# Router logits from column-tiled fp32 matmuls and one transposition, in a sandwich of linear attention and a gated expert layer

## The chip, the cores and the metric

The kernel runs on one core of one Trainium2 chip. The metric is the device time of one execution in microseconds (us); lower is better. Engines are named as the profile names them: PE is TensorE's matmul stream and PEld its weight loads, DVE is VectorE, ACT is ScalarE, POOL is GpSimd, SP issues the DMAs.

## The reference, cut to what matters

Input is x of 2 x 4096 tokens with 256 features. The first half adds a chunked linear attention, the second a layer of 8 experts weighted by a router. The part that the change touches is the router:

```python
x = x + _layernorm(attention(_layernorm(x)))
x = x + _layernorm(experts(_layernorm(x)))

# inside experts: x is (tokens, 256), Wr is (256, 8)
inh = jax.nn.sigmoid(x @ Wr / temperature)
in_zone = (inh >= GOLDEN_LOWER) & (inh <= GOLDEN_UPPER)
dist = jnp.abs(inh - GOLDEN_CENTER)
w = jnp.exp(-dist / 0.1) * in_zone      # else: the two nearest experts by exp(-dist / 0.3)
out = sum over e of w[e] * ((silu(x @ Wg[e]) * (x @ Wu[e])) @ Wd[e])
```

## The kernel before, in words

The tokens are cut into 16 blocks of 512 (two batch rows of 256 tokens), and a block into four token tiles of 128. The loop bodies are written out by hand for each engine and tied together with counting semaphores: `reach(engine, counter, block, k)` waits until the k-th event of that block has happened. Tokens lie on the 128 partitions for the attention's rows, and features on the partitions for the operands of the expert layer: `ft_hi` and `ft_lo` hold the normalised rows transposed, [128 features, 2 halves of the features, 512 tokens], as a rounded high part and the rest, both in the type fp32r, which TensorE reads in one pass.

The order on PE is a software pipeline. While block f runs through the experts 2 to 7, the attention of the next block a is cut into steps (the table `STEPS`) that are set between the expert matmuls. One slot of the pipeline is `up(e, m)` (twelve matmuls of 512 columns into `gate_ps` and `up_ps`), a step of attention, `down(e - 1, m)` (twelve of 256 columns), and another step. At the end of `rest` stands the passage that the change touches: `up(0, 0, a)`, the router step of block a, `down(7, 0, f)`, `up(0, 1, a)`, `down(7, 1, f)`. Then `first_expert` begins with the transpositions `xt` of the block after that.

The router step (lines 532 to 538) takes each token tile as the stationary operand (a weight load of 128 columns) and streams 16 columns of router weights past it: the eight high parts and the eight low parts (`wr_hl`), or high parts and zeros (`wr_h0`) for `ft_lo`. That is 4 tiles x 2 feature halves x 2 parts = 16 matmuls. ACT copies the 64 columns of result out of PSUM (`rz`), POOL adds the two halves (`router_logit`), ACT takes tanh of the sum (`router_tanh`), and POOL and DVE work out the weights (`routing`, `route_rank`, `route_weights`).

The attention steps and the router share two halves of a PSUM region, `att_ps`. A step takes the half by its number in the block (`number_of`, even or odd), and waits until the result of the step two before it has been read (`READ_OUT`). The router is number 20, so it has the even half.

Three other steps use TensorE in smaller tiles, and the prediction speaks of them: `s` (line 472) and the second part of `o` (line 494) run fp32 matmuls in 64 x 64 tiles, four different tiles in turn; the first part of `o` (line 485) runs fp32 matmuls with 128 rows and 64 columns, two column tiles in turn. An fp32 matmul is two records in the trace (8 matmuls of line 485 are 16 records, 32 of line 472 are 64). `warm` (line 604) runs full 128 x 128 fp32 matmuls at the start. In the names of a matmul the moving operand stands first and the stationary one second.

Of the kernel before, what the change touches and what calls it, by code (L numbers as in the profile page):

```python
# [113 lines left out]
              ("wo", 1): 4, ("ft", 0): 10, ("ft", 1): 14}  # L114
ROUTER = ("r",)


def psum_steps(steps):
    return [s for after in steps for s in after
            if s[0] in ("xt", "q", "kv", "kt", "s", "o", "su", "ot", "wo", "ft")] + [ROUTER]  # L120

# [5 lines left out]
def build_program(nc, x, wq_t, wkv_t, wo_t, norm_w, wg, wu, wd, wr, temperature, out):  # L127
# [4 lines left out]
    with ctx:  # L132
# [11 lines left out]
        wo_hi, wo_lo = sb("wo_hi", [P, HG, HID], f32r), sb("wo_lo", [P, HG, HID], f32r)  # L144
        wr_raw = sb("wr_raw", [P, KT, E])
        wr_hl = sb("wr_hl", [P, KT, 2 * E], f32r)
        wr_h0 = sb("wr_h0", [P, KT, 2 * E], f32r)
        nw = sb("nw", [P, HG])
# [49 lines left out]
        euler = sb("euler", [P, TILES, E])  # L198
        rz = sb("rz", [P, TILES, 2, E])
        logit, tanh, inh = (sb(n, [P, TILES, E]) for n in ("logit", "tanh", "inh"))  # L200
        off, neg_off, dist, zone, below = (sb(n, [P, TILES, E]) for n in ("off", "neg_off", "dist", "zone", "below"))
# [49 lines left out]
        rz_copied = counter("rz_copied", 1)  # L251
        logit_ready = counter("logit_ready", 1)
        tanh_ready = counter("tanh_ready", 1)
# [20 lines left out]
        wo_scaled = sem("wo_scaled")  # L274
        wr_hi_ready = sem("wr_hi_ready")
        wr_ready = sem("wr_ready")
# [17 lines left out]

        READ_OUT = {ROUTER: (rz_copied, 1)}
        for n in range(KT):
# [17 lines left out]
        def number_of(step, a):  # L314
            return psum_order(a).index(step)
# [57 lines left out]
        def _(sp):  # L373
# [14 lines left out]
            sp.dma_start(nw[:, :], norm_w).then_inc(small_loaded, 16)  # L388
            sp.dma_start(wr_raw[:, :, :], wr.rearrange("(k p) n -> p k n", p=P)).then_inc(small_loaded, 16)
            sp.dma_start(temp[:, :], temperature.partition_broadcast(P)).then_inc(small_loaded, 16)  # L390
# [19 lines left out]
        def _(pe):  # L410
# [10 lines left out]
            def att_step(step, a):  # L421
# [97 lines left out]
                elif kind == "wo":  # L519
                    p = step[1]  # L520
                    reach(pe, ot_ready, a, p + 1)
                    for b in range(B):
                        last = products(dst[:, b, :],
                                        [((ot_hi[:, b, g * P:g * P + P], ot_lo[:, b, g * P:g * P + P]),
                                          (wo_hi[:, g, :], wo_lo[:, g, :])) for g in range(HG)])
                elif kind == "ft":
                    p = step[1]
                    reach(pe, x1n_ready, a, p + 1)
                    for k in range(KT):
                        for t in range(2):  # L530
                            last = nc.tensor.transpose(dst[:, k, t * P:t * P + P], rows[:, 2 * p + t, k * P:k * P + P], ident[:, :])
                elif kind == "r":
                    reach(pe, ft_ready, a, 2)
                    for t in range(TILES):
                        cols, ts = dst[:, 0, t * 2 * E:(t + 1) * 2 * E], slice(t * P, t * P + P)
                        for k in range(KT):
                            nc.tensor.matmul(cols, ft_hi[:, k, ts], wr_hl[:, k, :], start=k == 0, stop=False)
                            last = nc.tensor.matmul(cols, ft_lo[:, k, ts], wr_h0[:, k, :], start=False, stop=k == KT - 1)
                last.then_inc(att_done[0], 1)
# [46 lines left out]
            def rest(a, f):  # L586

                for e in range(2, E):
                    for m in range(MT):
                        up(e, m, f)  # L590
                        attention(4 * e - 4 + 2 * m, a)
                        down(e - 1, m, f)
                        attention(4 * e - 3 + 2 * m, a)
                up(0, 0, a)
                att_step(ROUTER, a)
                down(E - 1, 0, f)
                up(0, 1, a)
                down(E - 1, 1, f)
# [19 lines left out]
            up(0, 0, (0, 0))  # L618
            pe.wait_ge(wr_ready, 1)
            att_step(ROUTER, (0, 0))  # L620
            up(0, 1, (0, 0))
            pe.wait_ge(w_ready, ATT_W + UNITS)
            first_expert((1, 0), (0, 0))
# [18 lines left out]
        def _(act):  # L642
# [18 lines left out]
            def att_step(step, a):  # L661
# [45 lines left out]
                elif kind == "r":  # L707
                    reach(act, logit_ready, a, 0)
                    copy(rz[:, :, :, :], src[:, 0, 0:TILES * 2 * E].rearrange("p (t a e) -> p t a e", t=TILES, a=2))\
                        .then_inc(rz_copied[0], 1)  # L710

            def router_tanh(a):
                reach(act, logit_ready, a, 1)
                reach(act, dist_ready, a, 0)
                nc.scalar.activation(tanh[:, :, :], logit[:, :, :], ACT.Tanh, scale=half_inv_t[:, 0:1])\
                    .then_inc(tanh_ready[0], 1)

# [54 lines left out]
            def rest(a, f, more=True):  # L772
# [10 lines left out]
                if more:  # L783
                    normalise_x((a[0], a[1] + 1))
                silu(0, 1, a)
                router_tanh(a)
                high(0, 1, a)
# [9 lines left out]
            copy(wo_hi[:, :, :], wo_raw).then_inc(w_hi_ready, 1)  # L797
            act.wait_ge(small_loaded, 48)
            copy(wr_hl[:, :, 0:E], wr_raw[:, :, :])
            copy(wr_h0[:, :, 0:E], wr_raw[:, :, :])  # L800
            nc.scalar.activation(wr_h0[:, :, E:2 * E], wr_raw[:, :, :], ACT.Copy, scale=0.0).then_inc(wr_hi_ready, 1)
            for n, steps in enumerate(FIRST_STEPS):
# [33 lines left out]
        def _(dve):  # L836
# [162 lines left out]

            x_stats((0, 0))  # L1000
            nc.vector.memset(state[:, :, :, :, :], 0.0)
            settle(nc.vector.memset(v_sb[:, :, :, D:VA], 1.0))
# [12 lines left out]
            low(wo_lo[:, :, :], wo_raw, wo_hi[:, :, :]).then_inc(w_ready, 1)  # L1015
            dve.wait_ge(wr_hi_ready, 1)
            low(wr_hl[:, :, E:2 * E], wr_raw[:, :, :], wr_hl[:, :, 0:E]).then_inc(wr_ready, 1)
            settle(nc.vector.reciprocal(half_inv_t[:, :], temp[:, :]))
# [79 lines left out]
        def _(pool):  # L1098
# [33 lines left out]

            def router_logit(a):
                reach(pool, rz_copied, a, 1)
                nc.gpsimd.tensor_tensor(logit[:, :, :], rz[:, :, 0, :], rz[:, :, 1, :], ALU.add).then_inc(logit_ready[0], 1)

            def routing(a):
# [44 lines left out]
            for steps in FIRST_STEPS:  # L1182
                for step in steps:
                    att_step(step, (0, 0))
            router_logit((0, 0))
            x_root((1, 0))
# [3 lines left out]
            with pool.Fori(1, BLOCKS - 1) as i:  # L1190
                for n in range(4, len(STEPS)):
                    attention(n, (i, 0))
                x_root((i, 1))
                router_logit((i, 0))
                routing((i, 0))
# [5 lines left out]
            for n in range(4, len(STEPS)):  # L1201
                attention(n, (BLOCKS - 1, 0))
            router_logit((BLOCKS - 1, 0))
            routing((BLOCKS - 1, 0))
# [36 lines left out]
```

## Time and profile before

| | us |
|---|---|
| median of 3 runs (lowest, highest) | 1549.72 (1548.35, 1550.36) |
| the profiled execution | 1550.57 |
| its span, first to last instruction | 1548.9 |
| PE busy in the span | 1514.9 (98%) |
| DVE busy | 1005.0 (65%) |
| ACT busy | 683.1 (44%) |
| POOL busy | 446.4 (29%) |
| DMA, mean of the 16 engines over the span | 4.9% |

The 1.7 us between the profiled execution's time and its span lie before the first and after the last recorded instruction. Except in the first 85 us and the last few, PE is busy in every fortieth of the span and the granted clock is full. A busy share counts an engine as busy while any of its records is open, and matmul records overlap; so start to start times of PE say more than durations do.

### The profile page before, as it was taken

The numbers are of one execution on the slowest core, as the hardware profiler recorded it, in microseconds if no ns is written. First come the engines' busy times: TensorE is split into PE (matmuls) and PEld (weight loads), VectorE is DVE, ScalarE is ACT, GpSimd is POOL, SyncE is SP. The second block draws the span as 40 slices with busy tenths as digits, with TensorE's granted clock in tenths as the row PEclk, the third lists the DMA queues.
The fourth block names the chain that finished last, engine by engine and source line by source line (L and its number), as shares of the span: only waits on it lengthen the run. The fifth ranks groups of instructions, "written<-read, shape, count | busy, mean of one in ns | idle before, by whom it ended". The sixth has DMA issues, their size and how long they took to land. (4 is left out here: it accounts for less than half of the span.)

```text
span 1548.9 us, 35779 instructions
## 1 busy us (share of the span) xinstructions
PE 1514.9 (98%) x13648; PEld 1308.9 (85%) x13648; DVE 1005.0 (65%) x2388; ACT 683.1 (44%) x1264; POOL 446.4 (29%) x720
## 2 busy tenths in 40 slices
PE   7799999999999999999999999999999999999997
PEld 6688888888888888888888888888888888888886
DVE  4656656666666666756666666666666666666665
ACT  4543444445344453534445344453535445344433
POOL 1422413224141232413224141232413224141231
PEclk9999999999999999999999999999999999999999
DMA  4300000000000000000000000000000000000000
GB/s 116 103 1 2 28 0 14 14 14 14 0 14 14 14 14 0 27 0 14 14 14 14 0 14 14 14 14 0 24 3 14 14 14 14 0 14 16 1 8 21
DMA packets 25343, 24.56 MB, mean 16 GB/s; under 512 B 2016, under 2 KB 25056, under 8 KB 25312
## 3 DMA queue, kind: packets, MB, share of 16 engines
q1 hardware_dynamic: 25312, 24.13, 4.8%
q8 instruction: 21, 0.34, 0.1%
q14 instruction: 10, 0.08, 0.0%
HBM read 15.74 MB, written 8.39 MB: 16 GB/s over the span
## 5 line engine op out<-in xcount | busy, mean ns | idle before, releaser
L927 DVE TENSOR_TENSOR late<-late,up_ps 128x512 f32<-128x512 f32 x256 | 175.1, 684 | 173.2 <-PE up_ps L418 142.4
L418 PE MATMUL down_ps<-w_hi,h_hi 128*128 128x256 f32 x976 | 266.7, 295 | 0.0
L1130 POOL TENSOR_TENSOR rms_f<-rms_in,minus_half 128x16 f32<-128x16 f32 x32 | 93.7, 2929 | 588.8 <-DVE rms_in L891 588.8
L726 ACT ACTIVATE late<-gate_ps 128x512 f32<-128x512 f32 x256 | 152.2, 595 | 241.5 <-PE gate_ps L418 235.5
L418 PE MATMUL down_ps<-w_hi,h_lo 128*128 128x256 f32 x976 | 253.4, 281 | 0.0
L644 ACT ACTIVATE h_hi<-late 128x512 fp32r<-128x512 f32 x256 | 160.7, 628 | 189.2 <-DVE late L927 189.2
L949 DVE SCALAR_TENSOR_TENSOR late<-down_ps,route,late 128x256 f32<-128x256 f32 x364 | 158.9, 478 | 105.0 <-PE down_ps L418 102.4
L843 DVE TENSOR_TENSOR h_lo<-late,h_hi 128x512 fp32r<-128x512 f32 x256 | 175.8, 687 | 75.5 <-ACT h_hi L644 75.5
L418 PE MATMUL gate_ps<-ft_hi,w_hi 128*128 128x512 f32 x512 | 203.8, 398 | 0.6 <-ACT ft_hi L644 0.4
L418 PE MATMUL up_ps<-ft_hi,w_hi 128*128 128x512 f32 x512 | 203.8, 398 | 0.0
L418 PE MATMUL up_ps<-ft_hi,w_lo 128*128 128x512 f32 x512 | 203.1, 397 | 0.0
L418 PE MATMUL gate_ps<-ft_hi,w_lo 128*128 128x512 f32 x512 | 202.1, 395 | 0.0
L418 PE MATMUL down_ps<-w_lo,h_hi 128*128 128x256 f32 x976 | 195.9, 281 | 0.0
L418 PEld LDWEIGHTS down_ps<-w_hi,h_hi 128*128 128x128 f32 x976 | 183.5, 188 | 6.5
L418 PEld LDWEIGHTS down_ps<-w_hi,h_lo 128*128 128x128 f32 x976 | 184.9, 189 | 3.4
L418 PE MATMUL gate_ps<-ft_lo,w_hi 128*128 128x512 f32 x512 | 162.4, 398 | 0.0
L418 PE MATMUL up_ps<-ft_lo,w_hi 128*128 128x512 f32 x512 | 160.7, 395 | 0.0
L418 PEld LDWEIGHTS down_ps<-w_lo,h_hi 128*128 128x128 f32 x976 | 149.7, 188 | 0.0
L1106 POOL TENSOR_TENSOR shift<-mv,minus_one 128x2 f32<-128x2 f32 (+1 forms) x112 | 23.4, 209 | 335.1 <-DVE mv L851 335.1
L418 PEld LDWEIGHTS up_ps<-ft_lo,w_hi 128*128 128x128 f32 x512 | 97.2, 190 | 23.5
L418 PEld LDWEIGHTS up_ps<-ft_hi,w_hi 128*128 128x128 f32 x512 | 96.8, 189 | 23.8
L418 PEld LDWEIGHTS up_ps<-ft_hi,w_lo 128*128 128x128 f32 x512 | 96.7, 189 | 23.5
(159 smaller groups left out, 2667.3 us busy)
## 6 DMA issues: line engine op xcount, KB each, us to landing
xs<-in_x SPq DMA_DIRECT2D x32, 256.0 KB, 2.8
out_rows<-late SPq DMA_DIRECT2D x32, 256.0 KB, 2.2
late<-in_wg SPq DMA_DIRECT2D x8, 256.0 KB, 2.9
late<-in_wu SPq DMA_DIRECT2D x8, 256.0 KB, 2.8
late<-in_wd SPq DMA_DIRECT2D x8, 256.0 KB, 2.8
late<-in_wkv_t SPq DMA_DIRECT2D x1, 512.0 KB, 5.5
late<-in_wq_t SPq DMA_DIRECT2D x1, 256.0 KB, 4.4
late<-in_wo_t SPq DMA_DIRECT2D x1, 256.0 KB, 5.0
```

The source lines that it names most:

```text
L418: last = nc.tensor.matmul(dst, lhs, rhs, start=n == 0, stop=n == len(terms + low_terms) - 1)
L644: return nc.scalar.activation(dst, src, ACT.Copy)
L726: nc.scalar.activation(h_f[:, m, :], gate_ps[:, :], ACT.Silu).then_inc(silu_ready[0], 1)
L843: return nc.vector.tensor_tensor(dst, src, high_part.bitcast(f32), ALU.subtract)
L927: nc.vector.tensor_tensor(h_f[:, m, :], h_f[:, m, :], up_ps[m][:, :], ALU.mult).then_inc(h_ready[0], 1)
L949: last = nc.vector.scalar_tensor_tensor(dst[:, t, :], src, route[:, t, e:e + 1], acc[:, t, :], ALU.mult, ALU.add)
L1106: nc.gpsimd.tensor_tensor(shift[:, tiles], mv[:, tiles, 0], minus_one[:, tiles], ALU.mult)
L1130: nc.gpsimd.tensor_tensor(rms_f[:, p, :, :], rms_in[:, :, :], minus_half[:, :, :], ALU.pow)\
```

## The change

The router weights become the stationary operand. `wr_pad` holds them in plain fp32, padded with zeros from 8 to 32 columns. For each feature half and each part of the tokens, four matmuls follow each other, one for each token tile: each streams 128 tokens past `wr_pad` and writes 32 partitions of one PSUM bank, the four at partitions 0, 32, 64 and 96. The result has experts on partitions and tokens along the row. ACT copies it to `rz` (now 128 x 128), TensorE transposes it once (a new step `rt`, number 21, on the odd half), and ACT takes tanh directly from PSUM. The high and low copies of the router weights, their preparation at the start, and POOL's addition are gone. tanh moves ahead of `silu(0, 1)` on ACT.

```diff
-ROUTER = ("r",)
+ROUTER, ROUTER_T = ("r",), ("rt",)
...
-        wr_raw = sb("wr_raw", [P, KT, E])
-        wr_hl = sb("wr_hl", [P, KT, 2 * E], f32r)
-        wr_h0 = sb("wr_h0", [P, KT, 2 * E], f32r)
+        wr_pad = sb("wr_pad", [P, KT, D])
...
-        READ_OUT = {ROUTER: (rz_copied, 1)}
+        READ_OUT = {ROUTER: (rz_copied, 1), ROUTER_T: (tanh_ready, 1)}
...
                 elif kind == "r":
                     reach(pe, ft_ready, a, 2)
-                    for t in range(TILES):
-                        cols, ts = dst[:, 0, t * 2 * E:(t + 1) * 2 * E], slice(t * P, t * P + P)
-                        for k in range(KT):
-                            nc.tensor.matmul(cols, ft_hi[:, k, ts], wr_hl[:, k, :], start=k == 0, stop=False)
-                            last = nc.tensor.matmul(cols, ft_lo[:, k, ts], wr_h0[:, k, :], start=False, stop=k == KT - 1)
+
+                    for n, (k, part) in enumerate((k, part) for k in range(KT) for part in (ft_hi, ft_lo)):
+                        for t in range(TILES):
+                            last = nc.tensor.matmul(dst[D * t:D * t + D, 0, 0:P], wr_pad[:, k, :],
+                                                    part[:, k, t * P:t * P + P].bitcast(f32), start=n == 0, stop=n == 2 * KT - 1)
+                elif kind == "rt":
+                    reach(pe, rz_copied, a, 1)
+                    last = nc.tensor.transpose(dst[:, 0, 0:P], rz[:, :], ident[:, :])
...
                 att_step(ROUTER, a)
                 down(E - 1, 0, f)
+                att_step(ROUTER_T, a)
                 up(0, 1, a)
...
             pe.wait_ge(wr_ready, 1)
+            pe.wait_ge(small_loaded, 48)
             att_step(ROUTER, (0, 0))
             up(0, 1, (0, 0))
+            att_step(ROUTER_T, (0, 0))
...
                 elif kind == "r":
-                    reach(act, logit_ready, a, 0)
-                    copy(rz[:, :, :, :], src[:, 0, 0:TILES * 2 * E].rearrange("p (t a e) -> p t a e", t=TILES, a=2))\
-                        .then_inc(rz_copied[0], 1)
+                    copy(rz[:, :], src[:, 0, 0:P]).then_inc(rz_copied[0], 1)
...
             def router_tanh(a):
-                reach(act, logit_ready, a, 1)
-                reach(act, dist_ready, a, 0)
-                nc.scalar.activation(tanh[:, :, :], logit[:, :, :], ACT.Tanh, scale=half_inv_t[:, 0:1])\
-                    .then_inc(tanh_ready[0], 1)
+                reach(act, att_done, a, number_of(ROUTER_T, a) + 1)
+                reach(act, fallback_ready, a, 0)
+                logit = att_half(ROUTER_T, a)[:, 0, 0:P].rearrange("p (t e) -> p t e", t=TILES)[:, :, 0:E]
+                nc.scalar.activation(tanh[:, :, :], logit, ACT.Tanh, scale=half_inv_t[:, 0:1]).then_inc(tanh_ready[0], 1)
...
+                router_tanh(a)
                 silu(0, 1, a)
-                router_tanh(a)
                 high(0, 1, a)
...
-            act.wait_ge(small_loaded, 48)
-            copy(wr_hl[:, :, 0:E], wr_raw[:, :, :])
-            copy(wr_h0[:, :, 0:E], wr_raw[:, :, :])
-            nc.scalar.activation(wr_h0[:, :, E:2 * E], wr_raw[:, :, :], ACT.Copy, scale=0.0).then_inc(wr_hi_ready, 1)
...
             x_stats((0, 0))
+            nc.vector.memset(wr_pad[:, :, E:D], 0.0).then_inc(wr_ready, 1)
...
-            dve.wait_ge(wr_hi_ready, 1)
-            low(wr_hl[:, :, E:2 * E], wr_raw[:, :, :], wr_hl[:, :, 0:E]).then_inc(wr_ready, 1)
...
-            def router_logit(a):
-                reach(pool, rz_copied, a, 1)
-                nc.gpsimd.tensor_tensor(logit[:, :, :], rz[:, :, 0, :], rz[:, :, 1, :], ALU.add).then_inc(logit_ready[0], 1)
```

On PE, in the loop, the router before the change, between `up(0, 0)` and `down(7, 0)` (`wr_hl` and `wr_h` are the moving router weights):

```order
L418 MATMUL up_ps<-ft_lo,w_hi 128x512
L537 MATMUL att_ps<-wr_hl,ft_hi 128x16 [waits ft_ready]
L538 MATMUL att_ps<-wr_h,ft_lo 128x16
L537 MATMUL att_ps<-wr_hl,ft_hi 128x16
...
L538 MATMUL att_ps<-wr_h,ft_lo 128x16
L292 REGISTER_ALU [waits h_lo_ready]
L418 MATMUL down_ps<-w_hi,h_hi 128x256 [waits down_read]
```

The same place of PE after the change, to the first matmul of `up(0, 1)`:

```order
L414 MATMUL up_ps<-ft_lo,w_hi 128x512
L533 MATMUL att_ps<-ft_hi,wr_pad 32x128 [waits ft_ready]
L533 MATMUL att_ps<-ft_hi,wr_pad 32x128 x3
L533 MATMUL att_ps<-ft_lo,wr_pad 32x128 x4
L533 MATMUL att_ps<-ft_hi,wr_pad 32x128 x4
L533 MATMUL att_ps<-ft_lo,wr_pad 32x128 x4
L288 REGISTER_ALU [waits h_lo_ready]
L414 MATMUL down_ps<-w_hi,h_hi 128x256 [waits down_read]
...
L414 MATMUL down_ps<-w_lo,h_hi 128x256 x2
L288 REGISTER_ALU [waits ft_ready]
L537 MATMUL att_ps<-ident,rz 128x128 [waits rz_copied]
L288 REGISTER_ALU [waits ft_hi_ready]
L414 MATMUL gate_ps<-ft_hi,w_hi 128x512 [waits silu_ready]
```

There are 16 router matmuls in both. The transposition of `rz` is new, behind `down(7, 0)`, and waits for ACT's copy.

On ACT, in the loop, from the copy of the router's result on, before the change (`rows<-xs` is the normalisation for the next block, `late<-gate_ps` is silu(0, 1)):

```order
L644 ACTIVATE rz<-att_ps 128x64 [waits logit_ready,att_done]
L644 ACTIVATE h_hi<-late 128x512 [waits down_done,h_ready]
L292 REGISTER_ALU
L650 ACTIVATE rows<-xs,shift,rstd 128x256 [waits rstd1_ready] x4
L292 REGISTER_ALU
L726 ACTIVATE late<-gate_ps 128x512 [waits h_lo_ready,gate_done]
L292 REGISTER_ALU
L715 ACTIVATE tanh<-logit,half_inv_t 128x32 [waits dist_ready,logit_ready]
L644 ACTIVATE h_hi<-late 128x512 [waits down_done,h_ready]
```

And after the change:

```order
L646 ACTIVATE rz<-att_ps 128x128 [waits att_done]
L646 ACTIVATE h_hi<-late 128x512 [waits down_done,h_ready]
L288 REGISTER_ALU
L652 ACTIVATE rows<-xs,shift,rstd 128x256 [waits rstd1_ready] x4
L288 REGISTER_ALU
L716 ACTIVATE tanh<-att_ps,half_inv_t 128x32 [waits fallback_ready,att_done]
L288 REGISTER_ALU
L726 ACTIVATE late<-gate_ps 128x512 [waits h_lo_ready,gate_done]
L646 ACTIVATE h_hi<-late 128x512 [waits down_done,h_ready]
```

tanh now stands ahead of silu(0, 1) and waits for the transposition instead of for POOL's sum.

## Rows read from the trace of the kernel before

**Rows 1.** The page: busy time, share of the span and instructions of each engine.
```profile
PE 1514.9 (98%) x13648; PEld 1308.9 (85%) x13648; DVE 1005.0 (65%) x2388; ACT 683.1 (44%) x1264; POOL 446.4 (29%) x720
```

**Rows 2.** Busy us and records by stretch (PE, PEld, DVE, ACT, POOL), clock, DMA.
```profile
166.00:259.00 93.00, 92.86 (x845) 80.18 (x845) 61.62 (x148) 41.49 (x77) 28.12 (x44) 1.00 0.04 11
```

**Rows 3.** Who PE waited for: us in total, times, longest us.
```profile
PE att_ps L531 <- ACT rows L650: 6.0, 2, 3.8
```

**Rows 4.** Groups of PE by line: busy us, mean ns, idle before.
```profile
L538 PE MATMUL att_ps<-wr_h,ft_lo 128*128 128x16 f32 x128 | 29.1, 256 | 0.0
L537 PE MATMUL att_ps<-wr_hl,ft_hi 128*128 128x16 f32 x128 | 27.7, 246 | 0.0
```

**Rows 5.** Timeline of PE around one router step: start us, us, what.
```profile
538.18 0.62 PE L418 MATMUL up_ps<-ft_lo,w_hi 128*128 128x512 f32 x2
538.65 0.17 PE L537 MATMUL att_ps<-wr_hl,ft_hi 128*128 128x16 f32 x1
...
540.24 0.26 PE L538 MATMUL att_ps<-wr_h,ft_lo 128*128 128x16 f32 x1
540.35 0.37 PE L418 MATMUL down_ps<-w_hi,h_hi 128*128 128x256 f32 x1
...
541.86 0.39 PE L418 MATMUL gate_ps<-ft_hi,w_hi 128*128 128x512 f32 x1
```

**Rows 6.** Timeline of PE around attention steps `o` and `s`, in smaller tiles.
```profile
488.82 0.63 PE L418 MATMUL up_ps<-ft_lo,w_hi 128*128 128x512 f32 x2
489.37 1.12 PE L485 MATMUL att_ps<-state,q_t 128*64 128x132 f32 x16
490.42 1.14 PE L494 MATMUL att_ps<-v_sb,rows 64*64 64x33 f32 x64
...
496.40 1.16 PE L472 MATMUL att_ps<-q_t,kz 64*64 64x64 f32 x64
497.50 0.38 PE L418 MATMUL down_ps<-w_hi,h_hi 128*128 128x256 f32 x1
...
499.04 0.39 PE L418 MATMUL gate_ps<-ft_hi,w_hi 128*128 128x512 f32 x1
```

**Rows 7.** Timeline of PE at the start: full fp32 matmuls.
```profile
63.78 1.95 PE L604 MATMUL gate_ps<-ident 128*128 128x128 f32 x16
```

**Rows 8.** Timeline of PE around the eight transpositions `xt`.
```profile
544.65 0.28 PE L418 MATMUL down_ps<-w_hi,h_hi 128*128 128x256 f32 x1
...
545.84 0.40 PE L418 MATMUL down_ps<-w_lo,h_hi 128*128 128x256 f32 x2
546.08 1.03 PE L439 MATMUL att_ps<-ident,rows 128*128 128x128 f32 x8
546.87 0.48 PE L418 MATMUL gate_ps<-ft_hi,w_hi 128*128 128x512 f32 x1
...
549.77 0.28 PE L418 MATMUL down_ps<-w_hi,h_hi 128*128 128x256 f32 x1
```

**Rows 9.** Timeline of ACT behind the same router step.
```profile
540.53 0.22 ACT L644 ACTIVATE rz<-att_ps 128x64 f32<-128x64 f32 x1 [2.48 <-PE att_ps L538]
...
542.09 2.08 ACT L650 ACTIVATE rows<-xs,shift,rstd 128x256 f32<-128x256 f32 x4 [0.82 <-POOL shift L1109]
544.08 0.58 ACT L726 ACTIVATE late<-gate_ps 128x512 f32<-128x512 f32 x1
544.55 0.31 ACT L715 ACTIVATE tanh<-logit,half_inv_t 128x32 f32<-128x32 f32 x1
```

**Rows 10.** Timelines of POOL, ACT and PE behind the first block's router.
```profile
74.54 0.25 POOL L1135 TENSOR_TENSOR logit<-rz 128x32 f32<-128x32 f32 x1 [7.86 <-ACT rz L644]
...
77.12 2.07 ACT L650 ACTIVATE rows<-xs,shift,rstd 128x256 f32<-128x256 f32 x4 [1.38 <-POOL shift L1109]
...
79.34 1.07 PE L439 MATMUL att_ps<-ident,rows 128*128 128x128 f32 x8 [2.23 <-ACT rows L650]
```

**Rows 11.** Timeline of ACT at the start, behind the weights' preparation.
```profile
19.50 0.60 ACT L644 ACTIVATE k_sb<-att_ps 128x512 f32<-128x512 f32 x1 [4.46 <-PE att_ps L418]
```

More of the change, by code:

```diff
@@ L114 @@
               ("wo", 1): 4, ("ft", 0): 10, ("ft", 1): 14}
-ROUTER = ("r",)
+ROUTER, ROUTER_T = ("r",), ("rt",)
 def psum_steps(steps):
     return [s for after in steps for s in after
-            if s[0] in ("xt", "q", "kv", "kt", "s", "o", "su", "ot", "wo", "ft")] + [ROUTER]
+            if s[0] in ("xt", "q", "kv", "kt", "s", "o", "su", "ot", "wo", "ft")] + [ROUTER, ROUTER_T]
 PSUM_STEPS, FIRST_PSUM_STEPS = psum_steps(STEPS), psum_steps(FIRST_STEPS)
@@ L198, in build_program @@
         euler = sb("euler", [P, TILES, E])
-        rz = sb("rz", [P, TILES, 2, E])
-        logit, tanh, inh = (sb(n, [P, TILES, E]) for n in ("logit", "tanh", "inh"))
+        rz = sb("rz", [P, P])
+        tanh, inh = (sb(n, [P, TILES, E]) for n in ("tanh", "inh"))
         off, neg_off, dist, zone, below = (sb(n, [P, TILES, E]) for n in ("off", "neg_off", "dist", "zone", "below"))
@@ L251, in build_program @@
         rz_copied = counter("rz_copied", 1)
-        logit_ready = counter("logit_ready", 1)
         tanh_ready = counter("tanh_ready", 1)
@@ L274, in build_program @@
         wo_scaled = sem("wo_scaled")
-        wr_hi_ready = sem("wr_hi_ready")
         wr_ready = sem("wr_ready")
@@ L388, in _ @@
             sp.dma_start(nw[:, :], norm_w).then_inc(small_loaded, 16)
-            sp.dma_start(wr_raw[:, :, :], wr.rearrange("(k p) n -> p k n", p=P)).then_inc(small_loaded, 16)
+            sp.dma_start(wr_pad[:, :, 0:E], wr.rearrange("(k p) n -> p k n", p=P)).then_inc(small_loaded, 16)
             sp.dma_start(temp[:, :], temperature.partition_broadcast(P)).then_inc(small_loaded, 16)
@@ L1184, in _ @@
                     att_step(step, (0, 0))
-            router_logit((0, 0))
             x_root((1, 0))
@@ L1193, in _ @@
                 x_root((i, 1))
-                router_logit((i, 0))
                 routing((i, 0))
@@ L1202, in _ @@
                 attention(n, (BLOCKS - 1, 0))
-            router_logit((BLOCKS - 1, 0))
             routing((BLOCKS - 1, 0))
```

## The prediction

> **What bounds the kernel now.** I read the page's busy shares first. PE is busy for 98% of the span and no other engine for more than 65% [rows 1]. The stretches say the same block by block: in 93 us of the steady part, one block of tokens, PE is busy for 92.86 us at the full clock, 2.4 GHz, while DVE has 61.62 and ACT 41.49 [rows 2]. Then I read whom PE waits for. The longest entry is 6.0 us in two waits, both in the start [rows 3]; in the loop the list has nothing. So from the second block to the last what counts is how much PE has to stream, and a microsecond taken from PE in a block is a microsecond of the time, 15 times over.
>
> The router is a small part of that. Its two groups hold 128 + 128 records, 16 in each of 16 blocks [rows 4]. Their busy time (29.1 + 27.7 us) overstates the cost, since records overlap. The timeline gives it: first router matmul at 538.65, first down matmul behind it at 540.35, so 1.70 us for 16 matmuls, and the last one starts at 540.24, so 0.106 us apart on average and 0.11 from the last one to what follows [rows 5]. They stream only 16 columns each, so the pace isn't the streaming. It is the load of 128 stationary columns, which each needs. 16 x 1.70 = 27 us of the time, 1.8%, is all that the router's matmuls can give.
>
> **What the change costs on PE.** The new step has 16 fp32 matmuls with 32 stationary and 128 moving columns. An fp32 matmul leaves two records, so there will be 32. The trace has fp32 matmuls in three shapes:
> - Full array, 128 moving columns: 16 records in 1.95 us, one record 0.275 long, so (1.95 - 0.275) / 15 = 0.112 us apiece [rows 7]. Both the load of 128 columns (0.11 by the router's pace) and the streaming may set this.
> - Two column tiles of 64, 132 moving columns: 16 records in 1.12 us, start to next start 1.05 us; (1.12 - 0.28) / 15 = 0.056 us apiece, 0.112 a pair [rows 6]. Half the full array's price at the same number of columns: two column tiles stream side by side, and a round costs what one record of the full array costs.
> - Four 64 x 64 tiles, 64 or 33 moving columns: 64 records in 1.16 and 1.14 us, (1.15 - 0.22) / 63 = 0.015 us apiece, 0.059 a round of four [rows 6]. Half the columns, half the round, four tiles at once; with 33 columns no faster, so there the 64 loaded columns set the pace, and the loads of the four tiles overlap too.
>
> From these, a round of four 32-column tiles with 128 moving columns costs 0.112 x 128 / 132 = 0.109 us if all four stream at once. 32 records are 8 rounds, as the 16 records of line 485 are 8 rounds of two. I take that step's 1.05 us from start to next start, less 8 x 0.003 for the fewer columns, plus 0.01 for two more staggered starts: 1.03 us. This includes what leaving a tile shape costs. The bounds, from the nearest rows: four at once 1.03; two at once 16 x 0.112 + 0.15 (1.05 - 8 x 0.112, the fixed part) = 1.94; one after the other 32 x 0.112 + 0.15 = 3.73. I take the first, since the row nearest to it (64 x 64 tiles) shows four at once, and line 485 shows column tiles that share all 128 rows working in parallel. What no row shows is four streams read from the same partitions; line 485 and the 64 x 64 tiles both have two.
>
> Going into tiles costs on the way in: the pair of 512-column matmuls before them starts at 488.82 and the tiles at 489.37, 0.55 us [rows 6], against 0.47 before the router (538.18 to 538.65) [rows 5]: +0.08. On the way out the down matmuls behind tiles take 1.54 us (497.50 to 499.04) [rows 6], behind the old router 1.51 (540.35 to 541.86) [rows 5]: +0.03. The step therefore gives 1.70 - 1.03 - 0.08 - 0.03 = 0.56 us per block.
>
> The transposition: the eight of xt take 0.79 us from start to next start (546.08 to 546.87), and the twelve 512-column matmuls behind them take 2.90 (546.87 to 549.77) [rows 8] against 2.79 for the same twelve in the router's slot (541.86 [rows 5] to 544.65 [rows 8]). That is 0.90 for eight. The pace inside is (1.03 - 0.27) / 7 = 0.108. One costs 0.90 - 7 x 0.108 = 0.14 us. Bounds: 0.03 (if only the bare gap stays) to 0.9.
>
> Net per block: 0.56 - 0.14 = 0.42 us. In 15 blocks 6.3 us.
>
> **Waits that come and go.** The transposition waits for ACT's copy. ACT is idle for 2.48 us before that copy [rows 9] and starts it 0.29 us after the last router matmul starts [rows 5]; 128 columns instead of 64 add at most its own 0.22 us again. So rz is there 0.29 + 0.44, some 0.7 us after that matmul, and the transposition stands behind 1.5 us of down matmuls: covered with 0.8 us to spare. Without that cover all of PE's queue, up(0, 1) first, would stand behind it. The tanh now stands ahead of silu(0, 1), behind the normalisation that ends at 544.1 [rows 9]; the transposition will be over by 542, so tanh waits for nothing and moves silu by about 0.2 us. PE writes gate_ps again only at 546.87 [rows 8], 2.2 us after silu's old end at 544.66, and DVE's multiplication has to wait for up(0, 1) anyway. Cost 0; if the cover failed, 0.2 us per block (3 us in all). The step xt 1 of the next block now waits for tanh: done by 544.5, wanted at 546. POOL loses 0.25 us per block with 70% idle: nothing. The queues of SP carry the same DMAs.
>
> **The start.** In the first block POOL adds the logits at 74.54 before it takes the root for the next block; ACT's normalisation starts at 77.12, and PE idles 2.23 us before 79.34 [rows 10]. So block 0's saving on PE disappears in that idle time. The root may start some 0.3 us earlier without the addition, but tanh, before the normalisation there too, now waits for a transposition behind up(0, 1). The idle time ends 0.2 us earlier, I estimate, with -0.3 to +0.5 as bounds. The three small ACT copies and one DVE operation that go stand before 4.46 us of idle time on ACT [rows 11]: nothing.
>
> Sum against the profiled execution: 1550.57 - 6.3 - 0.2 = 1544.1. That execution is 0.85 above the median of the runs, so on the median's scale 1543.2. I say 1543.3.
>
> **Where the notes speak against it.** Line 485's loads are hidden behind its streaming: a round of 0.112 leaves no room for 64 loaded columns besides (0.056 by the router's pace) [rows 5, 6]. The Trainium skill (TensorE: Matmul & The Clock Gate, "The mechanism") says that weight loads overlap running matmuls only when the row group differs, and here all four tiles use all rows; by that rule each round would grow by the load, and the result would be the partial case below. The trace disagrees with it for two column tiles. The same page ("Measured speedup vs the span model") has three column tiles of 32 at 2.38 times one, 79% of full packing. An estimate from that page: 16 x 0.224 / (4 x 0.79) + 0.15 = 1.28 us for the step, 0.17 saved per block, 1547. No row here shows three or four column tiles.
>
> **Rivals.**
> - Partial packing. A 32-column load costs 0.111 x 32 / 128 = 0.028 us; if every round pays it, 8 x 0.028 = 0.22 us is lost, 0.20 per block stays, and 15 x 0.20 + 0.2 = 3.2 us gives 1546.5; with a somewhat worse loss, 1548. For it: the first round in line 485 pays something like that. Against it: the later rounds, and the full array, don't.
> - Slower: only two streams at once. The place is the router step, the mechanism the read of the moving operand: four fp32 streams from the same 128 partitions, where the trace shows never more than two. Price 1.94 for the step: 1.94 + 0.08 + 0.03 + 0.14 - 1.70 = +0.49 per block, 15 x 0.49 = 7.4, so 1557. It decides from a step of 1.45 us on, 0.16 us a round, which is fewer than 2.8 tiles at once. Against it: four loads in parallel in the 64 x 64 shape.
> - The change doesn't do what it says: the four tiles run one after the other. 3.73 - 1.45 = +2.28 per block, 34 us, 1584. Line 485 speaks against it.
>
> **Chances and range.** Four at once, 0.66: 1543.3, its own range 1541 to 1546. Partial, 0.14: 1546.5 to 1548. Two at once, 0.13: 1557. One at a time, 0.03. Something unseen in the first or last block, 0.04, half of it no change and half slower. A change under 0.2%, 3.1 us, can't be told from none with this kernel. The first case and about half of the partial one are faster by more: 0.72; same 0.10; slower 0.18. The range takes in the first two cases and no change, 1540.5 to 1550.5, and leaves out 0.18. Its low end is the transposition at its bare gap (15 x 0.11 = 1.7 us) and the rest as forecast, rounded down for the start.
>
> **What would show it.** Line 533 with 512 records of shape 128*32, in rounds of four starts a few ns apart and rounds 0.11 us apart. From the first of them to the first down matmul 1.03 us (1.94 for two at once, 1.25 if loads show). Down matmuls of the slot 1.54 us. The transposition at line 537, 0.14 us on the way to up(0, 1), without an idle entry under ACT rz. The block's period shorter by 0.42 us. The prediction is wrong if the rounds are longer than 0.12 us, if PE shows waits for rz or tanh in the loop, or if a wait at the ft transpositions grows by what the router gave.

## The result, and the profile after

The changed kernel takes 1539.84 us (median of 6 runs, 1539.36 to 1541.07), the kernel before 1549.15 on the same chip (6 runs, 1548.34 to 1550.41). The ratio is 0.9941 [0.993, 0.9951]: 9.3 us less. I had forecast 1543.3 and a range from 1540.5 on. So the sign was right and the gain too small by three tenths: 6.5 forecast (6.3 in the loop, 0.2 at the start), 9.3 measured. All times in this document are of executions with the clock at full speed; one of the ten of e3_layout below took 2586 us at a granted clock of 0.68 and is left out.

The page's busy times, which answer to [rows 1]: PE is still the engine that is busy for 98% of the span. It has 256 router records and 16 transpositions more, and is busy 10.8 us less.

```profile
PE 1504.1 (98%) x13920; PEld 1288.0 (84%) x13920; DVE 1004.3 (65%) x2388; ACT 683.2 (44%) x1261; POOL 434.3 (28%) x704
```

The groups of PE by line and form (busy us, mean ns, idle before), which answer to [rows 4]. All 512 router records are of the form 128*32, and neither they nor the transposition have idle time ahead of them:

```profile
L533 PE MATMUL att_ps<-ft_hi,wr_pad 128*32 128x128 f32 x256 | 13.2, 279 | 0.0
L533 PE MATMUL att_ps<-ft_lo,wr_pad 128*32 128x128 f32 x256 | 12.9, 273 | 0.0
L537 PE MATMUL att_ps<-ident,rz 128*128 128x128 f32 x16 | 4.4, 272 | 0.0
```

The timeline of PE around the router step of the same block as in [rows 5] (start us, duration, what):

```profile
534.57 0.63 PE L414 MATMUL up_ps<-ft_lo,w_hi 128*128 128x512 f32 x2
535.13 0.43 PE L533 MATMUL att_ps<-ft_hi,wr_pad 128*32 128x128 f32 x8
535.37 0.40 PE L533 MATMUL att_ps<-ft_lo,wr_pad 128*32 128x128 f32 x8
535.59 0.40 PE L533 MATMUL att_ps<-ft_hi,wr_pad 128*32 128x128 f32 x8
535.81 0.40 PE L533 MATMUL att_ps<-ft_lo,wr_pad 128*32 128x128 f32 x8
536.14 0.39 PE L414 MATMUL down_ps<-w_hi,h_hi 128*128 128x256 f32 x1
...
537.68 0.27 PE L537 MATMUL att_ps<-ident,rz 128*128 128x128 f32 x1
537.71 0.48 PE L414 MATMUL gate_ps<-ft_hi,w_hi 128*128 128x512 f32 x1
...
540.59 0.28 PE L414 MATMUL down_ps<-w_hi,h_hi 128*128 128x256 f32 x1
```

The step is 536.14 - 535.13 = 1.01 us. Eight records are two rounds of four, and behind the first two rounds (0.24 us) the next eight start every 0.22 us: a round is 0.109, as forecast. How the other terms came out:

| term, us per block | forecast | measured | from |
|---|---|---|---|
| router step | 1.03 | 1.01 | 535.13 to 536.14 |
| entry into tiles | +0.08 | +0.09 | 534.57 to 535.13 = 0.56, before 0.47 [rows 5] |
| down run behind | +0.03 | +0.03 | 536.14 to 537.68 = 1.54, before 1.51 [rows 5]; the mean of thirteen blocks is 1.530 against 1.513, so +0.02 |
| transposition and what it does behind | 0.14 | 0.12 | 0.03 to 537.71, then 2.88 to 540.59, before 2.79 [rows 5, 8] |
| net, in the slot | 0.42 | 0.45 | 0.69 - 0.09 - 0.03 - 0.12 |

The waits, too: ACT copies rz at 536.28 and has the tanh at 539.92, ahead of silu and behind the normalisation (against [rows 9]); tanh starts about two us behind the end of the transposition, and silu at 540.09:

```profile
536.28 0.28 ACT L646 ACTIVATE rz<-att_ps 128x128 f32<-128x128 f32 x1 [1.85 <-PE att_ps L533]
...
537.93 2.08 ACT L652 ACTIVATE rows<-xs,shift,rstd 128x256 f32<-128x256 f32 x4 [0.86 <-POOL shift L1104]
539.92 0.26 ACT L716 ACTIVATE tanh<-att_ps,half_inv_t 128x32 f32<-128x32 f32 x1
540.09 0.57 ACT L726 ACTIVATE late<-gate_ps 128x512 f32<-128x512 f32 x1
```

So the slot (the router step with what stands directly around it) gave 0.45 x 15 = 6.7 us. Where are the other 2.6? I take as the period the time from one router step's first record to the next one's. The timeline of PE has them 13 blocks apart, in the kernel before:

```profile
166.52 0.17 PE L537 MATMUL att_ps<-wr_hl,ft_hi 128*128 128x16 f32 x1
...
1375.99 0.17 PE L537 MATMUL att_ps<-wr_hl,ft_hi 128*128 128x16 f32 x1
```

and in the kernel after:

```profile
165.50 0.32 PE L533 MATMUL att_ps<-ft_hi,wr_pad 128*32 128x128 f32 x4
...
1366.79 0.32 PE L533 MATMUL att_ps<-ft_hi,wr_pad 128*32 128x128 f32 x4
```

(1375.99 - 166.52) / 13 = 93.04 and (1366.79 - 165.50) / 13 = 92.41. The period fell by 0.63 us, 0.18 more than the slot. Those 0.18 lie in runs of twelve down matmuls (256 columns) that the change doesn't touch. One of them as an example. The one at 549.77 in the kernel before [rows 8] lasts until

```profile
551.21 0.40 PE L418 MATMUL gate_ps<-ft_hi,w_hi 128*128 128x512 f32 x1
```

1.44 us; in the kernel after the same run is 1.41 long (545.69 to 547.10):

```profile
545.69 0.28 PE L414 MATMUL down_ps<-w_hi,h_hi 128*128 128x256 f32 x1
...
547.10 0.40 PE L414 MATMUL gate_ps<-ft_hi,w_hi 128*128 128x512 f32 x1
```

Over thirteen blocks this run takes 1.435 us on average before and 1.417 after. A block has sixteen such runs. Added up, each from its first start to the start of what follows, they take 23.73 us before and 23.56 after, although the one behind the router grew by 0.02: 0.18 less in the other fifteen. (The 512-column matmuls outside the slot take 0.03 more, the attention's steps 0.03 less.) DVE and ACT do the same work in both kernels (61.6 and 41.5 us in a period, [rows 2] and below), so it isn't less traffic.

```profile
165.50:257.90 92.40, 92.24 (x862) 79.00 (x861) 61.64 (x148) 41.51 (x77) 26.98 (x43) 1.00 0.04 11
```

**Theory:** the place of buffers in SBUF. The change declares 256 bytes per partition for the router weights (wr_pad) where 320 stood (wr_raw 64, wr_hl 128, wr_h0 128), so xs and every buffer behind it starts 64 bytes lower: xs 96 bytes behind a multiple of 128 where it was 32. **Rivals** to it: the new slot shifts the engines against each other, so that they disturb PE's reads less; or the moved tanh does.

### The profile page after: what moved, and what is told of

The parts are those of the page before. It is cut to its first block and busy times, and to the rows that moved or that the text cites. A ratio compares the mean times of both kernels' runs of the same rounds, so it can differ in the third digit from the quotient of the medians.

```text
span 1539.4 us, 36292 instructions
## 1 busy us (share of the span) xinstructions
PE 1504.1 (98%) x13920; PEld 1288.0 (84%) x13920; DVE 1004.3 (65%) x2388; ACT 683.2 (44%) x1261; POOL 434.3 (28%) x704
## 5 line engine op out<-in xcount | busy, mean ns | idle before, releaser
L414 PEld LDWEIGHTS gate_ps<-ft_lo,w_hi 128*128 128x128 f32 x512 | 96.5, 188 | 23.8
```

Of the source, the lines that this page charges most:

```text
L414: last = nc.tensor.matmul(dst, lhs, rhs, start=n == 0, stop=n == len(terms + low_terms) - 1)
```

## The experiments

Every kernel ran beside the kernel before on its chip; the medians of the kernel before were 1549.0 to 1550.0 there, and the ratio is to those. "Period" is read as above, over 13 blocks of the profiled execution, and "step" is the mean of the router step in us.

| kernel | us, median | ratio to before | period | step |
|---|---|---|---|---|
| before | 1549.15 | | 93.04 | 1.70 |
| after | 1539.84 | 0.9941 [0.993, 0.9951] | 92.41 | 1.01 |
| e1_one_tile | 1562.08 | 1.0081 [1.0061, 1.0102] | 93.79 | 2.39 |
| e2_two_tiles | 1548.71 | 0.9993 [0.9983, 1.0003] | 92.87 | 1.47 |
| e3_layout | 1545.75 | 0.9979 [0.9969, 0.9989] | 92.86 | 1.70 |
| e4_half | 1530.66 | 0.9876 [0.9859, 0.9892] | 91.95 | 0.57 |
| e5_tanh_after_silu | 1539.61 | 0.994 [0.9923, 0.9957] | 92.41 | 1.01 |
| e6_aligned | 1539.53 | 0.9935 [0.9918, 0.9952] | 92.32 | 1.01 |
| e7_shift64 | 1542.14 | 0.9953 [0.9937, 0.997] | 92.54 | 1.01 |
| e8_full | 1532.49 | 0.9887 [0.987, 0.9903] | 91.94 | 0.57 |
| e9_both | 1530.63 | 0.9884 [0.9868, 0.9901] | 91.86 | 0.57 |
| e10_h_moved | 1541.91 | 0.9953 [0.9937, 0.9969] | 92.53 | 1.01 |
| e11_late_moved | 1539.99 | 0.9942 [0.9922, 0.9962] | 92.39 | 1.01 |

### Where the other 0.18 us is

**e3_layout**, the kernel before, its instructions untouched, with its buffers where the change puts them:

```
-        wr_raw = sb("wr_raw", [P, KT, E])
         wr_hl = sb("wr_hl", [P, KT, 2 * E], f32r)
...
-        logit, tanh, inh = (sb(n, [P, TILES, E]) for n in ("logit", "tanh", "inh"))
+        spare = sb("spare", [P, 64])
+        tanh, inh = (sb(n, [P, TILES, E]) for n in ("tanh", "inh"))
...
+        logit, wr_raw = sb("logit", [P, TILES, E]), sb("wr_raw", [P, KT, E])
```

> The kernel before, with only the places of small tensors in SBUF moved, so that every large buffer has the address that it has in the changed kernel (64 bytes lower per partition; wr_raw and logit now lie at the end, 256 spare bytes behind rz). It asks where the 0.18 us per block come from that the changed kernel gains outside the router slot, spread over its groups of 256-column matmuls. If addresses do it: period 92.85 instead of 93.03, time 1549.2 - 2.5 = 1546.7. If the place of the instructions or the work of other engines does it: 93.03 and 1549.2.

The period is (1371.37 - 164.25) / 13 = 92.86, 0.18 less than in the kernel before, and the run of down matmuls of above is 1.41 us long, as after (on average 1.412). All sixteen runs take 0.19 less than in the kernel before. Timeline of PE:

```profile
164.25 0.17 PE L538 MATMUL att_ps<-wr_hl,ft_hi 128*128 128x16 f32 x1
...
546.78 0.28 PE L419 MATMUL down_ps<-w_hi,h_hi 128*128 128x256 f32 x1
...
548.19 0.40 PE L419 MATMUL gate_ps<-ft_hi,w_hi 128*128 128x512 f32 x1
...
1371.37 0.17 PE L538 MATMUL att_ps<-wr_hl,ft_hi 128*128 128x16 f32 x1
```

So the place alone makes the missing part, with the router as it was and with every instruction as it was; the rival that the new slot shifts the engines isn't needed. From here to the kernel after the period falls by 0.45: that is the slot.

**e7_shift64**, the opposite: the kernel after, its large buffers back.

```
+        spare = sb("spare", [P, 16])
         xs = sb("xs", [P, TILES, HID])
```

> The kernel after with 64 unused bytes per partition ahead of xs, so that xs and every buffer declared behind it lie where they lay before the change; all instructions as after. Theory (the place of the large buffers in SBUF sets the pace of the 256-column matmuls, and gave 0.18 us of the 0.63 us per block): the period goes from 92.41 to 92.41 + 0.18 = 92.58 us and the time from 1539.8 to about 1539.8 + 15 x 0.18 = 1542.5; the mean run of twelve 256-column matmuls lies back near 1.373 us instead of 1.362. Rival (the place is not it; what e3_layout changed by its 0.18 was something else, as the order in which the small tensors lie): period 92.41, 1539.8 us. The router step stays at 1.01 us by either.

(1366.21 - 163.21) / 13 = 92.54, and the same run takes 1.43 us (on average 1.427):

```profile
163.21 0.32 PE L534 MATMUL att_ps<-ft_hi,wr_pad 128*32 128x128 f32 x4
...
543.93 0.28 PE L415 MATMUL down_ps<-w_hi,h_hi 128*128 128x256 f32 x1
...
545.36 0.39 PE L415 MATMUL gate_ps<-ft_hi,w_hi 128*128 128x512 f32 x1
...
1366.21 0.32 PE L534 MATMUL att_ps<-ft_hi,wr_pad 128*32 128x128 f32 x4
```

0.13 of the 0.18 are back, and the time is 2.3 us above after's, 1542.1. This is close to the kernel that I forecast, the change without the move, and it is 1.2 us from the 1543.3. The down matmuls have all of it back: their sixteen runs take 23.74 us. What didn't come back, 0.05, lies outside them, half of it in the attention's steps, and stays open; the small tensors behind the large ones don't stand as before here.

**e10_h_moved** and **e11_late_moved** ask which buffer it is. The same 64 spare bytes stand directly ahead of h_hi in the one, of late in the other (shown for e10):

```
+        spare = sb("spare", [P, 16])
         h_hi, h_lo = sb("h_hi", [P, 2, MT, TOK], f32r), sb("h_lo", [P, 2, MT, TOK], f32r)
```

> The kernel after with 64 unused bytes per partition directly ahead of h_hi, so that h_hi, h_lo, late and the small tensors lie where they lay with e7_shift64, and xs, rows, xt, q_t, shared, x1 and ft where they lie in after. It tells which of the moved buffers matters. Theory (the reads of h_hi and h_lo, which are the stationary operands of the 256-column matmuls that changed their pace): the whole 0.13 us is back, period 92.54 and 1541.8 us. Rival (the traffic of the other engines on the buffers of attention, xs to x1): period stays at 92.41, 1539.8 us.

> The kernel after with the 64 unused bytes directly ahead of late, so that h_hi and h_lo lie as in after, and only late (the float32 hidden values, the accumulator, the kept x1) and the small tensors are moved. Theory (h_hi and h_lo are what matters): period 92.41 us, 1539.8 us. Rival (DVE's and ACT's traffic on late disturbs the reads of PE, and its place sets how much): period 92.54 us, 1541.8 us.

Timelines of PE, first of e10:

```profile
164.31 0.32 PE L534 MATMUL att_ps<-ft_hi,wr_pad 128*32 128x128 f32 x4
...
545.03 0.28 PE L415 MATMUL down_ps<-w_hi,h_hi 128*128 128x256 f32 x1
...
546.47 0.40 PE L415 MATMUL gate_ps<-ft_hi,w_hi 128*128 128x512 f32 x1
...
1367.26 0.32 PE L534 MATMUL att_ps<-ft_hi,wr_pad 128*32 128x128 f32 x4
```

then of e11:

```profile
165.70 0.32 PE L534 MATMUL att_ps<-ft_hi,wr_pad 128*32 128x128 f32 x4
...
1366.70 0.32 PE L534 MATMUL att_ps<-ft_hi,wr_pad 128*32 128x128 f32 x4
```

With h_hi, h_lo and what stands behind them moved the period is 92.53 and the run 1.44 us; with only late and the small tensors moved the period is 92.39. All that e7 cost comes with the two buffers from which the down matmuls load their stationary operand. Neither the place of attention's buffers nor that of late matters.

ACT writes h_hi and DVE writes h_lo, so one rival is left that no run was made for: not PE's reads but these writes. The traces of e10 and after speak against it. The same instructions stand in both; from one down matmul to the next e10 takes 1.1 ns more on average (2288 places in thirteen blocks), and 1.0 ns more where neither of these writes goes on (1547 of them). Whether the place counts by itself or by its distance from the moving operand, w_hi and w_lo, which didn't move, no run tells.

**e6_aligned** is the kernel after with 32 spare bytes ahead of xs (`[P, 8]`), so that the large buffers start on multiples of 128.

> The kernel after with 32 unused bytes per partition ahead of xs, so that the large buffers start on multiples of 128 bytes (they start 96 bytes behind one in the kernel after, 32 bytes behind one in the kernel before). Theory A (a buffer that straddles a boundary is read slower, so aligned is at least as fast as after): period 92.41 us or less, 1539.8 us or less; if 64 bytes gave 0.18 us, up to as much again, 92.2 and 1537. Theory B (only the distance between the two operands of a matmul counts, and 96 happened to suit): anything between before's pace and after's, 92.41 to 92.58 us, 1539.8 to 1542.5.

(1365.42 - 165.31) / 13 = 92.32, 0.09 less than after:

```profile
165.31 0.32 PE L534 MATMUL att_ps<-ft_hi,wr_pad 128*32 128x128 f32 x4
...
1365.42 0.32 PE L534 MATMUL att_ps<-ft_hi,wr_pad 128*32 128x128 f32 x4
```

The period lies where theory A put it, but the down matmuls don't bear the theory out. I compare runs of twelve from first to last start (fourteen of a block's sixteen; the other two follow matmuls of the same shape): 1.368 us here, against 1.362 after and 1.373 before. The gain is in the 512-column matmuls, twelve of which take 2.563 against 2.580. So "aligned is faster" is too simple, and why the two shapes answer differently stays open. The time, 1539.53, doesn't tell 0.09 us per block from none.

**e5_tanh_after_silu** puts the tanh back behind silu(0, 1).

> The changed kernel with tanh back behind silu(0, 1) on ACT, as before the change. If tanh's place is worth nothing (as predicted): period 92.41, time 1539.8. If the earlier tanh is the source of the 0.18 us per block outside the router slot: period 92.6, time 1542.5.

The period is 92.41, after's, and the time 1539.61. That rival falls: the tanh's place is worth nothing that could be measured.

### What the column tiles do

**e1_one_tile** runs the four tiles one after the other:

```
-                    for n, (k, part) in enumerate((k, part) for k in range(KT) for part in (ft_hi, ft_lo)):
-                        for t in range(TILES):
+                    for t in range(TILES):
+                        for n, (k, part) in enumerate((k, part) for k in range(KT) for part in (ft_hi, ft_lo)):
```

> The changed kernel with its 16 router matmuls in another order: all four of token tile 0 first, then those of tile 1, and so on, so that consecutive matmuls use the same 32-column tile. Same work, same result. Theory (four column tiles stream side by side, and a record of 128 fp32 columns occupies its tile for 0.11 us): 32 records one after the other, the step goes from 1.01 us to about 3.6 (32 x 0.112, less a little overlap where the tile changes), the block's period from 92.41 to 95.0, the time to about 1579. Rival (the gain is only that 32 stationary columns load faster than 128, and the tiles don't matter): step stays near 1.0, time 1540.

**e2_two_tiles** runs tiles 0 and 1 together, then 2 and 3, with a loop `for pair in range(2)` outside and `for t in (2 * pair, 2 * pair + 1)` inside.

> The changed kernel with the router matmuls in the order tiles 0, 1, 0, 1, ... and then 2, 3, 2, 3, ... Theory: two tiles at a time, 16 rounds of 0.112, step 1.9 us, period 93.3, time about 1553. It is the price that the slower rival of the prediction put on two streams at once (1.94). Rival (tiles don't matter): 1540.

The timelines of PE at the step, of e1:

```profile
540.90 0.41 PE L533 MATMUL att_ps<-ft_hi,wr_pad 128*32 128x128 f32 x2
...
541.36 0.41 PE L533 MATMUL att_ps<-ft_hi,wr_pad 128*32 128x128 f32 x4
...
543.29 0.39 PE L414 MATMUL down_ps<-w_hi,h_hi 128*128 128x256 f32 x1
```

and of e2:

```profile
537.39 0.41 PE L534 MATMUL att_ps<-ft_hi,wr_pad 128*32 128x128 f32 x4
...
537.85 0.43 PE L534 MATMUL att_ps<-ft_hi,wr_pad 128*32 128x128 f32 x8
...
538.86 0.39 PE L414 MATMUL down_ps<-w_hi,h_hi 128*128 128x256 f32 x1
```

The order is as both theories had it: the fewer tiles stand side by side, the longer the step. Both sizes missed, and by one thing. The rows in the middle have twice the records of the first in the same 0.22 us: around a change of tile PE already works on the next one. With 1.01 - 8 x 0.109 = 0.14 for what isn't rounds, e1's 2.39 are 20.7 rounds in place of 32, over three changes, and e2's 1.47 are 12.2 in place of 16, over one: 3.8 rounds overlap per change in both. A round is one record in e1 and two in e2. So matmuls of different tiles also overlap when they don't directly alternate: the next tile starts beside the fourth-last round of the tile or pair ahead of it. That is four records ahead in the one and eight in the other, so it isn't a fixed number of records, and what sets it no run here shows. In the kernel after all four tiles alternate and overlap throughout.

**e4_half** leaves the products of ft_lo out of the router step (`enumerate((k, ft_hi) for k in range(KT))`).

> The kernel after without the products of ft_lo in the router step (half of its matmuls are left out, which leaves the low part out of the logits). It prices a round of four column tiles. Theory (the 8 rounds of 0.109 us are the step, and the way in and out is fixed): four rounds fewer, 4 x 0.109 = 0.44 us, so a step of 1.01 - 0.44 = 0.57 us, a period of 92.41 - 0.44 = 91.97 and 1539.8 - 15 x 0.44 = 1533.2 us. Rival (a large part of the step is the change of the tile shape, which hides in the rounds): the step falls by less than 0.44, the rest of it shows behind, 0.2 to 0.3 us per block and 1535 to 1537 us.

The step is 0.57 (531.83 to 532.41 below): 0.44 less for four rounds, so 0.109 a round and 0.14 fixed, and nothing of it shows behind.

```profile
531.83 0.64 PE L533 MATMUL att_ps<-ft_hi,wr_pad 128*32 128x128 f32 x16
532.41 0.39 PE L414 MATMUL down_ps<-w_hi,h_hi 128*128 128x256 f32 x1
```

The period is 91.95, 0.45 less than after, so 6.8 us in 15 blocks. The time fell by 9.2. What remains is paid once, as the two profiled executions show: in the kernel after PE stands still for 0.76 us ahead of one matmul in the block after the loop, and here it doesn't:

```profile
1388.33 0.50 PE L414 MATMUL gate_ps<-ft_hi,w_lo 128*128 128x512 f32 x1 [0.76 <-issue]
```

and the second router step starts at 164.02 in place of 165.50. The place of that start differs between profiled executions of kernels whose start is almost alike (162.72 in e5, 165.50 in after), so I don't count it as a gain of e4.

### A version faster than both

**e8_full** leaves nothing out, but multiplies ft as one fp32 operand instead of two parts:

```
-                    reach(pe, ft_ready, a, 2)
-                    for n, (k, part) in enumerate((k, part) for k in range(KT) for part in (ft_hi, ft_lo)):
+                    reach(pe, ft_full_ready, a, 2)
+                    for k in range(KT):
...
+                elif kind == "ft_full":
+                    p = step[1]
+                    reach(act, ft_ready, a, p + 1)
+                    copy(ft_full[:, :, p * 2 * P:(p + 1) * 2 * P], att_half(("ft", p), a))\
+                        .then_inc(ft_full_ready[0], 1)
```

> A version meant to be faster than both. Nothing is left out: ACT copies ft from PSUM once as plain fp32 into rows, which is free then, and the router step takes its 8 k-steps from that copy, 32 stationary by 128 moving columns, instead of 16 from ft_hi and ft_lo. The fp32 matmul multiplies in full precision, so the high and low parts need not be multiplied apart. Theory (PE is the bound, the copies lie in ACT's idle time): as without the low products, a step of 0.57 us, a period of about 91.97 and 1533.3 us; ACT's busy time grows by 2 copies of about 0.6 us per block. Rival (the copies come on the way to something that PE waits for): the second ft copy delays the normalisation or the silu behind it on ACT, or the router waits for the copy, by up to 0.6 us per block; then 0.44 - 0.6 = -0.16, and the time is 1542.

Timeline of ACT, then of PE, then a period by stretch:

```profile
530.25 0.63 ACT L647 ACTIVATE h_hi<-late 128x512 fp32r<-128x512 f32 x1
530.77 1.17 ACT L647 ACTIVATE rows<-att_ps 128x512 f32<-128x512 f32 x2
532.55 0.60 ACT L732 ACTIVATE late<-gate_ps 128x512 f32<-128x512 f32 x1 [0.61 <-PE gate_ps L416]
```

```profile
533.84 0.64 PE L534 MATMUL att_ps<-rows,wr_pad 128*32 128x128 f32 x16
534.42 0.39 PE L416 MATMUL down_ps<-w_hi,h_hi 128*128 128x256 f32 x1
```

```profile
166.06:258.00 91.94, 91.78 (x846) 78.55 (x845) 61.57 (x148) 42.69 (x79) 26.84 (x43) 1.00 0.04 11
```

ACT works 1.18 us more per period, and behind the two copies it still has 0.61 us of idle time before silu: the rival falls. PE starts the step 1.9 us after the copies end and loses nothing. The result, 1532.49, is the theory's 1533.3 within a microsecond. As in e4, the stop of 0.76 us isn't there, which the theory didn't have.

**e9_both** adds e6's 32 bytes.

> The kernel of e8_full (router from one fp32 copy of ft, nothing left out) with the large buffers on multiples of 128 bytes as in e6_aligned. Theory (the two gains are in different matmuls and add): period 91.945 - (92.407 - 92.318) = 91.86 us, time 1532.5 - 15 x 0.09 = 1531.2 us. Rival (the aligned placement gives nothing with the other pace of the slot, since it only shifts when engines meet in SBUF): period 91.94, 1532.5 us.

```profile
164.25 0.32 PE L535 MATMUL att_ps<-rows,wr_pad 128*32 128x128 f32 x4
...
1358.48 0.32 PE L535 MATMUL att_ps<-rows,wr_pad 128*32 128x128 f32 x4
```

The period is (1358.48 - 164.25) / 13 = 91.86, 0.08 less than e8's. So the two gains add by the period. The times don't tell e8 and e9 apart: 1530.63 against 1532.49, on two chips, with ratios whose intervals cover each other. Both leave nothing out and are 1.1 to 1.2% under the kernel before.

## Why the prediction was right, and where it failed

- **Four tiles at once: right.** 1.03 forecast, 1.01 measured; the rivals with two (1.94) or one (3.73) needed a step that no run shows, and even e2 (1.47) and e1 (2.39) stay below them. The 64 x 64 rows [rows 6] were the right neighbours, although here four streams come from the same partitions.
- **Loads that show: fell.** Rounds stay at 0.109 us, and a step with half the rounds is 0.44 shorter. The Trainium skill (TensorE: Matmul & The Clock Gate, "The mechanism") has, in its list of what overlaps, weight loads overlap running matmuls only where the row group differs, though the text ahead of the list also allows a background weight buffer. In these rows all four tiles use all rows and the loads are hidden, so the trace disagrees with the rule of the list. It does for the full array as well: down matmuls start 0.12 us apart, and the load of 128 columns that each needs, 0.11 us by the old router's pace [rows 5], is hidden behind the one ahead.
- **Entry, way out, transposition: right to 0.02 us each.** They were read as distances from start to start around similar steps. A matmul's own record doesn't tell them: the transposition's is 0.27 us long, and it cost 0.12. The change of tile shape costs 0.09 on the way in and 0.02 to 0.03 behind.
- **No new waits: right.** In the loop PE waits for neither rz nor tanh. The list of waits now has the ft transpositions,

```profile
PE att_ps L527 <- ACT rows L652: 6.9, 16, 3.8
```

against 2 times in [rows 3], which looks like a wait that appeared. It grew by 0.02 us only: the second ft transposition starts 0.79 us behind the pair ahead of it now, and 0.77 before. The list leaves out idle times below 0.15 us; this one was 0.14 in every block of the loop and is 0.16 (in e3 too, where only the place of the buffers differs). My sentence that "in the loop the list has nothing" was true of the list and not of the loop.
- **The step that failed** is the frame of the sum: "Net per block: 0.56 - 0.14 = 0.42 us. In 15 blocks 6.3 us". It priced the slot and took the other 91 us of a block as unchanged, since the same instructions stand there. They are the same, but their operands aren't where they were: 64 bytes of declarations fewer moved h_hi and h_lo, and a block ran 0.18 us faster outside the slot, 2.7 us in 15 blocks (the time of e3 alone: 3.3 us, by its interval 1.7 to 4.8). The diff showed the cause in its first lines (wr_raw, wr_hl, wr_h0 out, wr_pad in), and I read them only as work. It had no term and no width in the range, whose low end was built from the transposition alone.
- **How the parts meet the 9.3.** 0.45 x 15 = 6.7 and 2.7 make 9.4, and that this is so near is partly luck. In the two profiled executions (9.5 apart) thirteen periods give 8.2 us, the part before the second router step 1.0 and the part behind the last one 0.7, while the one period in between, with the stop of 0.76 us, is 0.4 longer than before.
- **A slip in the chances.** By the shares given there, faster is 0.66 + 0.07 = 0.73 and same 0.07 + 0.02 = 0.09, not 0.72 and 0.10. Nothing hangs on it.
- **The start: not to be told.** The 0.2 us there drown in a start whose second router step lies anywhere from 162.7 to 166.5 us in the thirteen profiled executions.
- **The stop behind the loop had no term.** All eight kernels whose router step has 16 column-tiled matmuls show it once (after, e1, e2, e5, e6, e7, e10, e11), with 0.5 to 1.1 us; before, e3 and the three with 8 such matmuls (e4, e8, e9) don't. So it comes with the change, and it costs time where the forecast had nothing. The profile names nothing that PE waits for there, and what sets it is open.

## What to carry to other kernels

A step with few stationary columns should be priced by rounds: the number of k-steps times the price of one matmul of the streamed columns (0.218 us for an fp32 one of 128), if the tiles alternate in the queue. In this kernel 0.14 us came on top for the step itself, and about 0.12 around it for the change of tile shape. Once PE is the bound, read the declarations of a diff as well as its instructions: where a change adds or drops an SBUF tensor, run the kernel before with the new addresses, or the difference is put down to the wrong edit. And ask of a split operand whether the split is still needed: here, with 32 stationary columns, one full fp32 operand costs half of what its two parts did.

## What the runs showed of the hardware

- The place in SBUF of the buffers that hold a stationary operand changed the pace of its matmuls by about 1%. Runs of twelve with 256 columns (the fourteen of above, first to last start) take 1.373 to 1.375 us (before, e7, e10) or 1.360 to 1.362 (e3, after, e11), and h_hi and h_lo lie 64 bytes lower in the second group. In before and e3, and in e10 and after, everything else on PE is equal. The Trainium skill (SBUF — State Buffer, "Door 1: The DMA port swizzle", its note on cachelines) has an access pay where it crosses to a new 16-byte line. All the moves here are multiples of 16 bytes and so change nothing by that rule; the runs show a difference all the same. Which stage between SBUF and PE it comes from, no run here shows.
- In the kernel before the period alternated between 93.07 and 92.99 from block to block; in e3 and after by 0.01 at most. I don't know why.
- Four rounds of fp32 records overlap across a change of column tile even if the program runs one tile, or one pair of tiles, after the other (3.8 by the length of the step, in e1 and e2).
- The stop of 0.5 to 1.1 us, once and behind the loop, stands in the eight kernels with the longer router step and in none of the other five.
